# First attention in plain fp32: value products of two heads side by side, part of the probability tiles turned by DMA

## The reference, cut to what matters

```python
def _L0_xattn_ref(q, k, v, add_attn, mask, w_q, w_k, w_v, w_o, ln_g, ln_b):
    N_HEAD = 16; D_K = 64; D_V = 64
    qh = (q @ w_q).reshape(B, L, N_HEAD, D_K).transpose(0, 2, 1, 3)
    kh = (k @ w_k).reshape(B, L, N_HEAD, D_K).transpose(0, 2, 1, 3)
    vh = (v @ w_v).reshape(B, L, N_HEAD, D_V).transpose(0, 2, 1, 3)
    attn = jnp.einsum('bhqd,bhkd->bhqk', qh * scale, kh) + add_attn
    attn = jnp.where(mask == 0, NEG_INF, attn)
    attn = jax.nn.softmax(attn, axis=-1)
    out = jnp.einsum('bhqk,bhkd->bhqd', attn, vh)
    out = out.transpose(0, 2, 1, 3).reshape(B, L, N_HEAD * D_V)
    out = out @ w_o + residual      # then a layer norm
```

## Time and profile before

| | us |
|---|---|
| median of 3 runs | 4008.87 |
| lowest, highest | 4005.39, 4010.63 |
| the profiled execution | 4015.94 |
| its span | 4014.1 |

### The profile page before, as it was taken

How to read it: one execution, slowest core, us unless ns; L and a number is a source line. 1 busy time by engine, 2 the same in 40 slices (tenths; PEclk the granted TensorE clock), 3 DMA queues, 4 the chain that set the end, 5 groups by cost and what they waited for, 6 DMA issues and landing times.

```text
span 4014.1 us, 64482 instructions
## 1 busy us (share of the span) xinstructions
PE 3817.7 (95%) x21468; PEld 3007.7 (75%) x21468; DVE 2887.3 (72%) x6121; ACT 2428.7 (61%) x5300; POOL 1849.3 (46%) x1905
## 2 busy tenths in 40 slices
PE   9999999999999988999999998889999979999999
PEld 7888888888888875666666666666666658888887
DVE  7777777798888887888888787777878753333334
ACT  7666667666666666877777767777777741111111
POOL 4343334333433345667767666667666631001001
PEclk9999999999999999999999999999999989999999
DMA  4433433212111146666666547676666671011000
GB/s 137 142 126 116 142 116 119 74 61 62 65 56 56 63 137 166 171 175 167 166 164 158 145 127 192 184 187 180 166 172 167 167 232 62 35 37 55 32 32 32
DMA packets 587543, 486.09 MB, mean 121 GB/s; under 512 B 405968, under 2 KB 405968, under 8 KB 586192
## 3 DMA queue, kind: packets, MB, share of 16 engines
q1 hardware_dynamic: 569424, 431.63, 38.8%
q10 hardware_dynamic: 17792, 50.33, 3.6%
HBM read 197.68 MB, written 188.22 MB: 96 GB/s over the span
## 4 chain that ended last, share of the span: by engine, by line
PE 39%; ACT 8%; DVE 6%; issue 5%; DMA 2%; POOL 2%; SPq 0%; DVEq 0%; POOLq 0%; ACTq 0%
PE psV L1488 5%; PE psT L1442 4%; PE psS L1420 3%; PE psJ L1365 3%; PE psS L1365 3%; PE psS L1366 3%; PE psS L1367 3%; ACT PR L1774 3%; PE psJ L1367 3%; PE psJ L1366 3%; PE psT L1365 2%; PE psT L1367 2%; PE psT L1366 2%; POOL QS L2343 2%; DVE PR L1973 1%
## 5 line engine op out<-in xcount | busy, mean ns | idle before, releaser
L2343 POOL TENSOR_SCALAR QS<-QK 32x1024 fp32r<-32x1024 f32 (+2 forms) x1152 | 1236.8, 1074 | 863.5 <-DVE QK L1992 425.9
L1774 ACT ACTIVATE PR<-PR,MN 128x512 f32<-128x512 f32 x1536 | 1101.8, 718 | 374.8 <-DVE MN L1973 205.9
L1973 DVE CUSTOM_DVE_ANT_0 PR<-psS,RAW 128x512 f32<-128x512 f32 x1024 | 694.9, 682 | 301.7 <-PE psS L1417 191.8
L1442 PE MATMUL psT<-ID,PR 128*128 128x128 f32 x4680 | 712.9, 275 | 111.3 <-ACT PR L1774 102.9
L1442 PEld LDWEIGHTS psT<-ID,PR 128*128 128x128 f32 x4680 | 565.1, 141 | 268.9 <-ACT PR L1774 152.3
L1796 ACT ACTIVATE R<-psT 128x512 fp32r<-128x512 f32 x512 | 304.4, 595 | 323.9 <-PE psT L1442 322.3
L1420 PE MATMUL psS<-QS 128*128 128x512 f32 x1024 | 458.4, 448 | 20.0 <-DVE PR L1977 7.5
L1977 DVE TENSOR_SCALAR_CACHE_REDUCE PR<-psS 128x512 f32<-128x512 f32 x512 | 346.4, 683 | 120.8 <-PE psS L1420 117.5
L1816 ACT ACTIVATE PR<-psS,COLS 128x512 f32<-128x512 f32 x128 | 88.3, 690 | 547.0 <-PE psS L1367 537.6
L2088 DVE TENSOR_TENSOR R<-psT,R 128x512 fp32r<-128x512 f32 x512 | 349.3, 682 | 0.0
L2056 DVE CAST QK<-PR 128x512 fp32r<-128x512 f32 x128 | 59.2, 462 | 399.1 <-ACT PR L1816 353.8
(11 more groups left out here) (150 smaller groups left out, 8982.3 us busy)
## 6 DMA issues: line engine op xcount, KB each, us to landing
split_rows<-RAW SPq DMA_DIRECT2D x192, 256.0 KB, 2.7
split_rows<-plain SPq DMA_DIRECT2D x174, 256.0 KB, 2.5
x<-Y SPq DMA_DIRECT2D x96, 256.0 KB, 2.2
RAW<-x SPq DMA_DIRECT2D x96, 256.0 KB, 3.6
W<-kept ACTq DMA_DIRECT2D x12, 2048.0 KB, 11.1
Y<-x SPq DMA_DIRECT2D x96, 256.0 KB, 3.6
kept_c<-R SPq DMA_DIRECT2D x32, 512.0 KB, 5.0
kept<-ROWS SPq DMA_DIRECT2D x32, 512.0 KB, 3.0
```

The lines of the kernel that those rows point to most:

```text
L1442: mm = nc.tensor.transpose(dst[:, kt * P:(kt + 1) * P], prob(st, k)[:, kt * P:(kt + 1) * P], ID[:, :])
L1774: nc.scalar.activation(prob(st, k), prob(st, k), ACT.Exp, bias=MN[:, k % 8:k % 8 + 1], scale=-1.0, accum_out=row_sums(st, SM, g)[:, qt, j: ...
L1973: nc.vector.tensor_tensor_reduce(out=prob(st, k), in0=psS[:, n % 2], in1=FB[:, k % NT], scale=-st.scale, scalar=BIG, op0=ALU.add, op1=ALU. ...
L2343: nc.gpsimd.tensor_scalar(to, pair, 1.0, 1.0, ALU.mult, ALU.mult).then_inc(stacked, 1)
```

## The change

L0a and L0b are done the way SA and CA are. P and V are not split. A group is two heads: their products for one block of keys, 128x64 each, go to the lower and the upper 64 partitions of psV. J_HI of V, P_LO's subtraction, HEAD_LO and HEAD_SUM go; the second half of R becomes free, and a ring of four heads of turned tiles takes the place of PT. In L0a 16 of 32 tiles a batch (even ones) are sent through DRAM, in L0b 24 (all but the last of each head). Of the others one of each group of eight is copied by ACT and the rest by DVE. Of each eight tiles' splits, ACT does numbers 4 and 6 in L0a and 1, 4 and 6 in L0b, DVE does 0 and 2, or 0, 2 and 5. Since DVE no longer empties every tile's bank itself, MAX now waits until the tile that held its place in PR three tiles earlier has been turned or split. The place to which a split tile is parted lies in VALUES between the values, so that a bounce moves 256 runs of 1 KB and not 128 of 2 KB. The tables of SA and CA move single steps by up to a slot and a half, PV of two blocks of keys in SA among them.

```diff
-SENT = (0, 2, 4, 6, 8, 10)
-SPLIT_BY_ACT = (2, 8)
-COPIED_BY_ACT = (3, 7, 11, 12, 14)
+SENT = {"L0a": (0, 2, 4, 6), "L0b": (0, 1, 2, 4, 5, 6), "SA": (0, 2, 4, 6, 8, 10), "CA": (0, 2, 4, 6, 8, 10)}
+SPLIT_BY_ACT = {64: (1, 4, 6), 32: (2, 8)}
+COPIED_BY_ACT = {64: (3,), 32: (3, 7, 11, 12, 14)}
...
 WIDE = {
-    "SENT": (1, 2, 3, 5.6),
-    "PV": (8.5, 8.5, 10, 10), "HEAD_LO": 10.5, "HEAD_SUM": 11,
+    "SENT": (1, 1.5, 2.5, 3.5),
+    "PV": (8.75, 8.75, 10.25, 10.25),
+    "GATHER": 11,
...
 SECOND = {
-    "PV": (8, 8.5, 9.5, 10),
+    "PV": (8, 8.5, 10, 10),
...
         def halves(tile):
-            return (PLAIN[:, 0] if tile[0] == "SA" else FB)[:, n % 4].bitcast(U16)
+            if laid(stage_of[tile[0]]):
+                return VALUES[:, n % 4].rearrange("p (h two c) -> p h two c", h=2, two=2)[:, :, 1].bitcast(U16)
+            return (PLAIN[:, 0] if tile[0] == "SA" else FB)[:, n % 4].bitcast(U16).rearrange("p (h k) -> p h k", h=2)
...
-            def values(st, h, kt, b):
-                for p in range(2):
-                    mm = nc.tensor.matmul(psV[0:2 * dk], VAL[:, kt, 2 * dk * h:2 * dk * (h + 1)],
-                                          PT[h % 2][:, p, kt, :], start=(kt == 0 and p == 0),
-                                          stop=(kt == NT - 1 and p == 1))
...
             def group_values(st, g, kt, b):
-                    tiles = [(st.name, b, k) for k in range(4 * NT * g, 4 * NT * (g + 1))]
+                    tiles = [(st.name, b, k) for k in range(st.per_group * NT * g, st.per_group * NT * (g + 1))]
...
             def weight_hi(stage, kind, kt):
+                elif tal["j"].n:
+                    act.wait_ge(j_full, tal["j"].done(tal["j"].n - 1))
...
-            def head_lo(st, h):
-                nc.scalar.activation(OG[j * dk:(j + 1) * dk, :], psV[dk:2 * dk], ACT.Copy).then_inc(pv_half, 1)
...
             def largest(st, k, first, b):
-                before = grouped(st) and tile_before(st, b, k)
+                before = tile_before(st, b, k)
...
-            def head_sum(st, h):
-                nc.vector.tensor_tensor(og, psV[0:dk], og, ALU.add).then_inc(pv_evac, 1)
...
             def prob_lo(st, k, b):
-                nc.vector.tensor_tensor(lo, full, f32(hi), ALU.subtract).then_inc(t_evac, 1)
+                dve.wait_ge(t_full, turned_at[st.name, b, k])
+                nc.vector.tensor_copy(probs_of(ring(st, b, h), qt), full).then_inc(t_evac, 1)
```

More of the change, by code:

```diff
@@ L318 @@
 DRAIN_OUT = ((44, 44.5, 45, 45.5), (46, 46.5, 47, 47.5), (48.5, 49, 50, 50.5), (51.5, 52, 52.5, 53))
-DRAIN_PV = ((32, 33, 34, 34), (36, 37, 38, 38))
+DRAIN_PV = (36, 36.5, 37, 38)
 def sent(st, b):
-    if not grouped(st):
-        return ()
-    return tuple(k for k in range(16 if st.name == "SA" and b == B - 1 else st.steps) if k % 16 in SENT)
+    every = st.per_group * NT
+    return tuple(k for k in range(16 if st.name == "SA" and b == B - 1 else st.steps) if k % every in SENT[st.name])
 def timetable(st, table, b=0):
@@ L344, in timetable @@
         g, last = h // st.per_group, h % st.per_group == st.per_group - 1
-        if not grouped(st) or last:
+        if last:
             for kt in range(NT):
-                add(NT * h + table["PV"][kt], "PV", (g if grouped(st) else h, kt))
-        if not grouped(st):
-            for step in ("HEAD_LO", "HEAD_SUM"):
-                add(NT * h + table[step], step, h)
-        elif last:
+                add(NT * h + table["PV"][kt], "PV", (g, kt))
             add(NT * h + table["GATHER"], "GATHER", g)
@@ L381, in timetable @@
     return ev
-def grouped(st):
-    return st is not None and st.dk == 32
 def laid(st):
@@ L421, in last_batch @@
         late |= {("JOB", (("OUT", tt), part)): slot for tt, row in enumerate(DRAIN_OUT) for part, slot in enumerate(row)}
-        late |= {("PV", (6 + h, kt)): slot for h, row in enumerate(DRAIN_PV) for kt, slot in enumerate(row)}
+        late |= {("PV", (3, kt)): slot for kt, slot in enumerate(DRAIN_PV)}
+        late |= {("GATHER", 3): DRAIN_PV[3] + 0.5}
         late |= {("RECIP", 3): 33, ("SPREAD", 3): 34, ("GROUP_HI", 3): 41.5, ("GROUP_LO", 3): 41.5}
@@ L1081, in tile_before @@
         def tile_before(st, b, k):
+            i = STAGES.index(st) * B + b
+            last = STAGES[(i - 1) // B]
             if k in beside(st):
-                return (st.name, b - 1, ("R", NG - 1)) if b else None
-            mine = [n for n in range(st.steps) if n not in beside(st)]
+                return (st.name, b, ("R", 0)) if k == 15 else (last.name, (i - 1) % B, ("R", NG - 1)) if i else None
+            mine, others = ([n for n in range(s.steps) if n not in beside(s)] for s in (st, last))
             at = mine.index(k) - 3
-            return (st.name, b, mine[at]) if at >= 0 else (st.name, b - 1, mine[at + len(mine) // 3 * 3]) if b else None
+            return (st.name, b, mine[at]) if at >= 0 else (last.name, (i - 1) % B, others[at + len(others)]) if i else None
         order = weight_order()
@@ L1473, in group_values @@
                     n = tal["pv"].next()
-                    tiles = [(st.name, b, k) for k in range(4 * NT * g, 4 * NT * (g + 1))]
+                    tiles = [(st.name, b, k) for k in range(st.per_group * NT * g, st.per_group * NT * (g + 1))]
                     for copied in (t_evac, p_copied):
-                        pe.wait_ge(copied, max(evacuated[tile][1] for tile in tiles
-                                               if tile not in sent_at and evacuated[tile][0] is copied))
+                        own = [evacuated[tile][1] for tile in tiles if tile not in sent_at and evacuated[tile][0] is copied]
+                        if own:
+                            pe.wait_ge(copied, max(own))
                     through = [sent_at[tile] for tile in tiles if tile in sent_at]
@@ L1788, in prob_hi @@
                 h, qt = divmod(k, NT)
-                if grouped(st) and not by_act(st, k):
+                if not by_act(st, k):
                     return
@@ L1824, in run @@
                             tal["s"].mark("pairs")
-                    elif step == "SPLIT" and k % 16 in SPLIT_BY_ACT:
+                    elif step == "SPLIT" and split_by_act(st, k):
                         split_prob(st, k, batch + off if at is None else at)
@@ L2121, in run @@
                         prob_lo(st, k, batch + off if at is None else at)
-                    elif step == "SPLIT" and k % 16 not in SPLIT_BY_ACT:
+                    elif step == "SPLIT" and not split_by_act(st, k):
                         split_prob(st, k, batch + off if at is None else at)
```

229 lines of the change are left out of this document (110 added, 119 removed), and 199 rows, old and new, of tables (SEAM, THIRD, WIDE).

## The result

The changed kernel takes **4058.6 us** (median of 4 runs, 4053.2 to 4061.5) beside 4009.8 us for the kernel before on the same chip (median of 4, 4005.4 to 4011.8). The ratio is 1.0117, with a 95% interval from 1.0105 to 1.0129: 1.2% slower, where I had forecast 3820, 5% faster, and gave slower a chance of 0.04. The profiled execution has a span of 4057.4 us, 43.3 more than before.

A forecast was written before the change was run, and what follows sets the result against it. PE was taken as the bound in L0a and L0b; 221 us less PE work minus 32 us of coupling gave 189 us off the profiled 4015.9, so 3827, or 3820 for the median; range 3780 to 3905.

The forecast's parts named there:

- PE, transposes: L0a and L0b: each tile PE no longer turns saves 0.44 us, 7.0 us a batch in L0a and 10.6 in L0b.
- PE, value products: L0a and L0b: a plain fp32 piece of two key blocks costs 1.20 us, saving 5.0 us a batch.
- rival 2: L0a and L0b: a 64-column product streams twice as long, a piece 2.05 us, the kernel about 3905; chance 0.07.
- The rule weighed against it: L0a and L0b value products: plain at a quarter of transposes' rate, piece 3.8 us, 15.6 us a batch lost; discounted.
- What the coupling costs: Engines waiting on each other: 3.0 us a batch in L0b, 1.0 in L0a, 32 us over all batches.
- The sign that I had set: The forecast is wrong if PE waits more than 6 us a batch for anything.
- rival 1: L0a and L0b: the DMA engines become the bound, 1 KB packets adding 0.72 us a tile, 3943 us; chance 0.08.
- rival 3: Four places of split_rows, each held 20 us as landings stretch, make the kernel slower, 4158 us; chance 0.04.
- The new wait at MAX: On DVE: MAX waits for the tile three earlier to be turned or split; costed at nothing.
- SA and CA: Their moved table steps: nothing taken, 10 us either way; SA's moved key block saves 11 us at most.

The follow-up runs named there:

- e3: The changed kernel with no tile of L0a and L0b sent through DRAM, PE turning all 32 a batch: 4030.4 us, ratio 1.0039.
- e6: The changed kernel without the second head's value products for the last three blocks of keys in L0a and L0b: 4079.1 us (2 runs).
- e4: The changed kernel with the fetch of sent tiles in L0a and L0b one slot later (4.5 for 3.5): 4016.4 us, ratio 1.0005.
- e13: The changed kernel with only the value products of L0a and L0b one slot later, the fetch left in place: 4048.0 us, ratio 1.0091.
- e5: The changed kernel without the value products of the second and third block of keys in L0a and L0b: 4053.0 us, ratio 1.0088.
- e7: The changed kernel with both fetch and value products of L0a and L0b one slot later: 3989.8 us, ratio 0.9941.
- e11: e7 with 8 of 32 tiles a batch sent in L0a in place of 16, L0b keeping 24: 3972.0 us, ratio 0.9894.
- e1: The kernel before with only the tables of SA and CA taken from the changed kernel: 3982.6 us, ratio 0.9921.
- e10: e7 with fetch and value products of L0a and L0b both half a slot later still: 3986.6 us, ratio 0.9937.
- e12: e11 with 16 of 32 tiles a batch sent in L0b in place of 24, 8 in L0a: 3985.6 us, ratio 0.9925.
- e14: e11 with no tiles sent in L0a in place of 8, 24 in L0b: 3992.8 us, ratio 0.9946.

## Why the prediction was wrong

**PE, transposes: right.** 320 turned tiles gone were to bring 141 us. e3 and the changed kernel differ by just these tiles: 1455.3 less 1321.3 is 134 us of work, 0.42 us a tile where I had 0.44.

**PE, value products: the first step that failed.** It reads "So a piece of two blocks costs 1.20 us", a gain of 80 us. It measured 1.87 us to the next start and a loss of 26: 106 us off. I read the count in the earlier trace rows as products and not as passes, so that I took the eight records of one block for two blocks. The comparison with the transposes, which I gave as the reason for choosing 1.20, had the same hole: the rate of one pass is indeed that of a transpose, 0.43 us for 512 columns against 0.11 for 128, but a product has two of them. One look at the program's order beside the trace (4 products here, 8 records there) would have settled it before any run. As rival 2 I had about the right price for a wrong reason, a width of 64 columns. The width costs nothing: two blocks of keys take 1.86 us with four heads of 32 columns (SA, 1914.76 to 1916.62 us) and 1.87 with two heads of 64. Nor does the second head, as e6 shows. With only this term mended, the forecast would have been rival 2's 3905 or so, still 150 us too low.

**The rule weighed against it.** The trace had transposes pass a column at the rate of one pass of a product. The Trainium skill (TensorE: Matmul & The Clock Gate, Terms) has its transpose mode "4× faster for FP32", and does not say faster than what. By the rows a transpose is twice as fast as a plain product here (0.11 us against 0.21 for 128 columns), since that makes two passes. By that rule the piece would be 3.8 us; it was 1.87. Neither the rule nor my reading of the rows was right, and the measured value lies between.

**What the coupling costs: the second step that failed, and the larger one.** "I take 3.0 for L0b" and 1.0 for L0a, 32 us in all, from SA's ratio of DVE's load; it measured 137 us of idle PE and 48 of half clock, 185 in all, 153 us off. DVE's load was not the reason. Its load fell nearly as computed (63.9 us a batch predicted in L0b, 200.68 / 3 = 66.9 measured; ACT 50.3 and 53.2), and at 72% it is less loaded than before. A large part of the reason stands in the slots, which I had quoted and not worked through: `"SENT": (1, 1.5, 2.5, 3.5)` leaves one slot, some 2.4 us, between bounce and fetch, and the earlier trace rows had the bounce landing after 2.6 us. SP issues in order, so it stood at the fetch, and what is behind it in SP's list (context, residual, x) came later. SA has 2.6 slots there (5.6 less 3), of 1.7 us, 4.4 us in all. I wrote down "about one step of 2.4 between them in SP's order" as part of how long a place is held, and never asked who stands behind SP. The runs that show it are e4 (42 us for one slot), e13 (10 us without it) and e5 (115 us of PE's work removed, next to nothing gained). Fetch and products together explain 68 of the 185 us (e7). The rest hangs on the tiles sent too, since it is gone in e3, but its cause is open. The sign that I had set, PE waiting more than 6 us a batch, was there: it was idle for 7.4 us a batch in L0a's window and 8.4 in L0b's.

**The DMA engines (rival 1): the term was right.** The queue's rows in the windows of L0a and L0b, to be read beside the earlier trace rows:

```profile
q1 hardware_dynamic: 82164, 59.50, 74.6%
```

```profile
q1 hardware_dynamic: 104766, 54.36, 77.8%
```

In L0b 77.8% of 280.1 us is 217.9 us for three batches, of which 51.3 are L0b's own of before (18.8% of 272.5): 2.31 us for each of the 72 tiles, against my 2.33. In L0a it is 2.30. The packets of 1 KB added nothing that shows. The share stayed at 0.75 to 0.78 only because the batches were longer; in e11 it reaches 0.87 in L0b and PE runs at full clock for most of it. That the engines would be full, rival 1, did not come.

**The four places (rival 3): the sign, by another road.** Slower it was, but not because a place is held 20 us: landings took 3.2 (L0a) and 3.0 us (L0b) for the bounce and 3.3 for the transpose, near the 2.6 and 3.5 I used. SP waited for the landing itself, not for a place.

**The new wait at MAX: right.** In neither window does DVE wait at line 1997 for ACT or a split; its idle time there is PE's scores (48.6 us in three batches of L0b).

**SA and CA: outside the bounds.** I had 0 with 10 either way and measured -32 in the changed kernel, and -35.5 in e1. For SA I had priced the moved block of keys at 11 us at most; from its first to its last score SA took 893.7 us before and 882.8 after, 11 less (14 less in e1). A group's products now come in two pieces of two blocks each instead of three, so one change to products and back goes for every group. The timeline of PE in SA after has only such rows:

```profile
1914.76 1.92 PE L1529 MATMUL psV<-plain 128*32 128x512 f32 x16
...
1919.13 1.92 PE L1529 MATMUL psV<-plain 128*32 128x512 f32 x16
```

The other 21 us are CA's (920.4 to 899.0), from moves of half a slot to two slots (VAR's last one by two, where I had said at most a slot and a half) that I had not worked through; which of them brings it was not tried.

**The sum again.** Forecast -189 us of span. Value products +106, transposes +7, waits and clock +153, SA and CA -32: that makes +45, and the span shows +43.

**What stays open.** After the later slots 50 to 96 us of idle PE remain in L0a and L0b (e7, e10, e11, e12, e14). Most of it is spread over many small waits, but one wait is large: the one at L0b's last group, 8.1 us in e12, 11.7 in e11, 19.6 in e7. With the stretch at 1.2 GHz that begins in it, that is about a quarter of what e11 still loses. All slots tried apply to every batch alike, and none of the runs changed the steps where L0b ends. Whether a larger ring, or more places of split_rows, would take these waits away was not tried. Nor was a fetch from another engine's queue, which would take the stop off SP's list. Each of the 17 stretches at 1.2 GHz stood behind or in waits of PE, 1.8 to 11.7 us in all each time, and the stretches went with the waits (none in e3, none in e11's L0a). That it is a consequence and not a cause is argued from that, not shown by a run in which only the clock changes.

## What to carry to other kernels

Before pricing a matmul from a timeline, divide the trace's records by the products of the program's order: they need not be one to one. An engine that only issues DMAs is an engine with a list too. For every wait that a change puts on it, compare the slots in between with the landing time in the profile, and name what is queued behind. And where a change mixes a new scheme with retuned tables of other stages, run the tables alone; in the changed kernel they were the only gain. Look at the first and last batch of a stage as well as at its middle: the longest wait of PE was there.

## What the runs showed of the hardware

- A plain fp32 product with 512 columns of the moving side is two passes of 0.43 us, each with its own record; an fp32r product is one of 0.23 us. Unsplit fp32 so costs 0.86 us where the split form with two fp32r products costs 0.46 (four of them in 0.91). Because two heads share a pass it came near to even here: 26 us more over 16 batches.
- Products in two column groups of 64 (two heads) run fully side by side: leaving one out leaves the piece as long (e6, 1.86 us with four records, 1.87 with eight).
- Waits of a few us on PE cost more than themselves. With 146.0 us of idle time the changed kernel had 17 stretches at 1.2 GHz, which cost up to 47.8 us more; the kernel before, with 9.3 us idle, had none. Of the 115 us of work that e5 removed, 69 came back as idle time and 43 as such stretches. The Trainium skill (TensorE: Matmul & The Clock Gate, HAM oscillation — how this bites in real kernels) describes a loop that waits for a DMA in each turn and starts each next piece at the low clock; here it came once or so a batch, with PE busy 90% of the time.
- The landing of a bounce of 256 KB, 2.9 us at the median over the whole program, is what an in-order issuer pays if it waits for it. The Trainium skill (DMA: Bandwidth & Descriptors, Issuing engines are not separate DMA queues) says that issuing from several engines saves only the sequencer's time, "usually small relative to the DMA itself". In this kernel the time was not small: issuing held SP for 1.26 us for a transpose that landed in 3.3, and SP stood waiting at the fetch for 79.5 us in 285. One slot more before the fetch was worth 42 us; issuing from a second engine was not tried.
